# Mixing x on 64x64 quarters of TensorE, two blocks at a time, in a fused attention and FFN kernel on one Trainium2 core

## The reference, cut to what matters

```python
x = x + attention(mix(x, itok_B_0_15, L0_cond_weights))
x = x + ffn(quantized_linear(x, condB_codebook))

def mix(x, condition, weights):            # x: (64, 32, 512)
    W = weights[condition]                 # (64, 32, 32), one of 16 matrices for each batch entry
    return jnp.einsum('bct,bcd->bdt', x, W)
```

## Time and profile before

| | |
|---|---|
| median of 3 runs | 1451.32 us (1451.01 to 1451.55) |
| the profiled execution, its own time | 1450.27 us |
| span of that execution | 1448.4 us |
| PE busy | 1443.8 us, 100% of the span |
| PEld busy | 1200.6 us, 83% |
| DVE busy | 1079.1 us, 75% |
| ACT busy | 726.7 us, 50% |
| POOL busy | 746.3 us, 52% |

### The profile page before, as it was taken

How to read it: one execution, slowest core, us unless ns; L and a number is a source line. 1 busy time by engine, 2 the same in 40 slices (tenths; PEclk the granted TensorE clock), 3 DMA queues, 4 the chain that set the end, 5 groups by cost and what they waited for, 6 DMA issues and landing times.

```text
span 1448.4 us, 34721 instructions
## 1 busy us (share of the span) xinstructions
PE 1443.8 (100%) x14507; PEld 1200.6 (83%) x14507; DVE 1079.1 (75%) x1507; ACT 726.7 (50%) x1331; POOL 746.3 (52%) x530
## 2 busy tenths in 40 slices
PE   9999999999999999999999999999999999999999
PEld 8788888888888888888888888888888888888887
DVE  8788868687786777875478888867987667667663
ACT  7766676766766667676333333334432322222221
POOL 7668777777777877776345555514561111112100
PEclk9999999999999999999999999999999999999999
DMA  4211011110111011102443343447653334244230
GB/s 152 66 45 45 31 38 45 45 44 25 45 45 45 29 39 45 45 31 67 138 155 137 131 136 134 145 151 244 200 195 110 103 118 132 85 136 132 74 118 30
DMA packets 106989, 135.13 MB, mean 93 GB/s; under 512 B 6224, under 2 KB 89424, under 8 KB 106320
## 3 DMA queue, kind: packets, MB, share of 16 engines
q1 hardware_dynamic: 105968, 132.49, 27.7%
q10 hardware_dynamic: 864, 0.42, 0.1%
HBM read 86.75 MB, written 46.14 MB: 92 GB/s over the span
## 4 chain that ended last, share of the span: by engine, by line
PE 97%; DVE 1%; ACT 1%; DMA 0%; issue 0%; SPq 0%; DVEq 0%
PE bank L717 42%; PE bank L960 25%; PE bank L736 21%; PE bank L919 4%; PE bank L845 3%; PE bank L988 1%; PE bank L1006 1%; DMA qk<-in_x_nat 0%; PE bank L666 0%; DVE qreg L1708 0%; PE bank L1017 0%; PE bank L974 0%; ACT xs_hi L1160 0%; DVE wa L1624 0%; DVE sqst L1708 0%
## 5 line engine op out<-in xcount | busy, mean ns | idle before, releaser
L717 PE MATMUL bank<-xs_hi,wa 128*128 128x512 f32 x1792 | 563.3, 392 | 0.1
L1527 POOL TENSOR_TENSOR accr<-accr,sqst 128x512 f32<-128x512 f32 x248 | 353.2, 1435 | 147.7 <-ACT sqst L1197 107.5
L717 PEld LDWEIGHTS bank<-xs_hi,wa 128*128 128x128 f32 x1792 | 336.3, 188 | 74.1 <-DVE qk L1775 2.3
L717 PE MATMUL bank<-xs_lo,wa 128*128 128x512 f32 x896 | 348.7, 389 | 0.0
L960 PE MATMUL bank<-ot,wo_main 128*128 128x512 f32 x1344 | 316.4, 392 | 0.0
L960 PEld LDWEIGHTS bank<-ot,wo_main 128*128 128x128 f32 x1344 | 249.5, 188 | 52.6
L736 PE MATMUL bank<-wv,xs_hi 128*128 128x512 f32 (+1 forms) x1008 | 282.6, 366 | 0.1
L1624 DVE TENSOR_TENSOR wa<-wraw,wa 128x256 fp32r<-128x256 f32 (+1 forms) x160 | 157.0, 982 | 96.7 <-ACT wa L1106 95.0
L1322 ACT ACTIVATE ot<-bank,vec 128x256 fp32r<-128x256 f32 x256 | 100.3, 476 | 239.0 <-PE bank L960 146.6
L736 PEld LDWEIGHTS bank<-wv,xs_hi 128*128 128x128 f32 x1008 | 182.1, 189 | 32.9 <-issue 1.9
L717 PEld LDWEIGHTS bank<-xs_lo,wa 128*128 128x128 f32 x896 | 168.3, 188 | 33.2
(11 more groups left out here) (224 smaller groups left out, 1726.9 us busy)
## 6 DMA issues: line engine op xcount, KB each, us to landing
values_b<-v_spill SPq DMA_DIRECT2D x60, 512.0 KB, 4.9
wraw<-in_wqk SPq DMA_DIRECT2D x32, 512.0 KB, 3.5
v_spill<-qk SPq DMA_DIRECT2D x64, 256.0 KB, 2.3
v_spill<-sqst SPq DMA_DIRECT2D x64, 256.0 KB, 2.2
score_spill<-sqst SPq DMA_DIRECT2D x32, 256.0 KB, 2.0
wraw<-in_wv SPq DMA_DIRECT2D x16, 512.0 KB, 5.1
wraw<-score_spill SPq DMA_DIRECT2D x16, 512.0 KB, 4.0
spare<-in_wo SPq DMA_DIRECT2D x15, 512.0 KB, 4.8
```

What stands on the lines that cost most here:

```text
L717: ins = pe.matmul(dst[:, :], wa[:, col:col + P], xpart[:, j - 1, kt, n * CH:(n + 1) * CH], start=(first and k == 0), stop=(k == 5), skip_g ...
L1527: pool.tensor_tensor(a, a, sq_slot(count), ALU.add).then_inc(acc_done, 1)
```

## The change

The four 32x32 blocks of a tile's `mixw` lie inside its two diagonal 64x64 blocks. The change leaves out the two off-diagonal 64x64 parts, which are zero, and cuts each of the others once more by its features: `mix_tile(block, half, t)` does one half of a tile's tokens (64 rows of the array, 64 moving columns) as two matmuls of 64 stationary columns, for the lower and the upper 64 features. A matmul of before is four matmuls now, each on one 64x64 quarter of the array.

`mix_pair(one, other)` does two blocks at a time. For each of the four tiles it issues the upper rows of `one` (two quarters, one bank) and the lower rows of `other` (two quarters, another bank). Then PE waits on a semaphore of its own, `mix_crossed`, until all of that is done, and does the lower rows of `one` and the upper rows of `other`. Both blocks are reported to `mixed` at the end. `mix_group(3)` therefore waits for DVE's first difference before either of its first two blocks, and for t4 as well before either of its last two.

```diff
+            def mix_tile(block, half, t):
+
+                g, r, c, i = block
+                rows = slice(half * 64, (half + 1) * 64)
+                for d in range(2):
+                    ins = pe.matmul(mix_bank(g, r)[d * 64:(d + 1) * 64, t * P + half * 64:t * P + (half + 1) * 64],
+                                    x_in[c][rows, t, i * P + d * 64:i * P + (d + 1) * 64],
+                                    mixw[rows, c * TC + t, rows], start=True, stop=True)
+                return ins
+
+            def mix_pair(one, other):
+
                 for t in range(TC):
-                    ins = pe.matmul(mix_bank(g, r)[:, t * P:(t + 1) * P], x_in[c][:, t, i * P:(i + 1) * P],
-                                    mixw[:, c * TC + t, :], start=True, stop=True)
-                ins.then_inc(mixed, 1)
+                    mix_tile(one, 0, t)
+                    ins = mix_tile(other, 1, t)
+                ins.then_inc(mix_crossed, 1)
+                crossed[0] += 1
+                pe.wait_ge(mix_crossed, crossed[0])
+                for t in range(TC):
+                    first = mix_tile(one, 1, t)
+                    second = mix_tile(other, 0, t)
+                first.then_inc(mixed, 1)
+                second.then_inc(mixed, 1)
...
-                for i in range(KI):
-                    mix_block_of(i % 2, (0, 3)[i // 2] if c == 0 else (1, 2)[i // 2], c, i)
+                for i in (0, 2):
+                    r = (0, 3)[i // 2] if c == 0 else (1, 2)[i // 2]
+                    mix_pair((0, r, c, i), (1, r, c, i + 1))
...
                     pe.wait_ge(ld_x[1], 16)
-                    mix_block_of(g, 0, 1, kt)
-                    mix_block_of(g, 3, 1, kt + 2)
+                    mix_pair((g, 0, 1, kt), (g, 3, 1, kt + 2))
                     pe.wait_ge(ld_x[3], 16)
-                    mix_block_of(g, 1, 3, kt)
-                    mix_block_of(g, 2, 3, kt + 2)
+                    mix_pair((g, 1, 3, kt), (g, 2, 3, kt + 2))
                 else:
                     pe.wait_ge(x_act, x_act_at(2, 1))
-                    mix_block_of(g, 1, 3, kt)
                     pe.wait_ge(x_dve, x_dve_at(2, "t1"))
-                    mix_block_of(g, 0, 1, kt)
+                    mix_pair((g, 1, 3, kt), (g, 0, 1, kt))
                     pe.wait_ge(x_dve, x_dve_at(2, "l3"))
-                    mix_block_of(g, 2, 3, kt + 2)
                     pe.wait_ge(x_dve, x_dve_at(2, "t4"))
-                    mix_block_of(g, 3, 1, kt + 2)
+                    mix_pair((g, 2, 3, kt + 2), (g, 3, 1, kt + 2))
```

More of the change, by code:

```diff
@@ L336, in build @@
         mixed = sem("mixed")
+        mix_crossed = sem("mix_crossed")
         x_act = sem("x_act")
@@ L662, in _ @@
             warm_up(2)
-            def mix_block_of(g, r, c, i):
-                for t in range(TC):
-                    ins = pe.matmul(mix_bank(g, r)[:, t * P:(t + 1) * P], x_in[c][:, t, i * P:(i + 1) * P],
-                                    mixw[:, c * TC + t, :], start=True, stop=True)
-                ins.then_inc(mixed, 1)
+            crossed = [0]
+            def mix_tile(block, half, t):
[7 more added lines that the diff above has]
+            def mix_pair(one, other):
+                for t in range(TC):
+                    mix_tile(one, 0, t)
[8 more added lines that the diff above has]
+                second.then_inc(mixed, 1)
             def mix_chunk(c):
```

## The result

| | before | after |
|---|---|---|
| median | 1451.27 us (1450.19 to 1452.22, 15 runs) | 1454.28 us (1453.66 to 1454.98, 15 runs) |
| span of the profiled execution | 1448.4 us | 1453.2 us |
| PE busy | 1443.8 us | 1442.6 us |
| matmul records on PE | 14507 | 14891 |
| DVE, ACT busy | 1079.1, 726.7 us | 1081.4, 726.4 us |

The change is slower: +3.0 us, ratio 1.0021 with a 95% interval of 1.0013 to 1.0029. The forecast was 0.7 us faster.

A forecast was written before the change was run, and what follows sets the result against it. PE bounds the program (97% of the span), but ACT and DVE most of the mixing; so only 0.7 us of PE's 4.8 saved arrives. From the median of 1451.32 that gives 1450.6 us, range 1449.4 to 1452.8.

The forecast's parts named there:

- Four quarters at once: In PE's mixing, all four array quarters work together: a round 0.056 us, a pair of blocks 1.20 us instead of 1.80.
- The rival with two quarters at once: In the mixing only two quarters work together: a round 0.112, a pair 2.04 us, result 1453.5 us; chance 5%.
- The floor of 25 ns: PE starts at most one record per 25 ns: a round of the mixing 0.10 us, result 1452.8 us; chance 2%.
- How much of that arrives: Following the pairs, block (0, 1) starts on ACT 0.70 us earlier, and only that 0.70 reaches p1(2).
- the steps on pairs in groups 2 and 3: mix_group(2) takes 2.4 for 3.6 us, the surplus lost in waits; mix_group(3)'s second pair waits for t4, until 26.8.
- the cost of fetching the instructions: The change adds no transfer but that of instructions; the sum has no term for it.
- Instructions come too late: Three more instruction packets, about 1 us each; PE waits for one or two before pair 3: 1451.6 to 1452.6; chance 3%.
- The clock: Clock falls in PE's new pauses of 1.3 us; p1(0) and p2(0) take 2.75 us more: 1453.4; chance 2%.
- The sum: -0.7 us in 1450.27 us of the profiled execution, 1450.6 us against the median; nothing after the mixing is touched.
- The later steps of the forecast: p6(0) gains 1.4 us, p7(0)'s wait takes the surplus, group 3's waits leave the squares 0.7 us earlier.

The follow-up runs named there:

- chunk0_pairs: Kernel before with pairs on quarters for chunk 0 alone, eight warm-up matmuls left out, 23 tiny matmuls added in group 3; 1450.71 us beside 1451.35.
- the two variants: chunk0_pairs, and the same with the loads of chunks 1 and 3 issued only once the first pair is mixed; 1450.71 and 1450.51 us.
- pad16: Kernel before with 16 tiny matmuls (64 instructions) added after the gathering of the mixing matrices; 1466.31 us, +16.0.
- pause_cold: Kernel before with PE waiting for chunk 1 of x ahead of chunk 2's blocks, the array idle; 1455.27 us, +5.0.
- late_phased: late_pairs with 32 tiny matmuls (128 instructions) added in mix_group(3) where PE waits for DVE; 1451.34 us, +1.0 against the kernel before.
- late_pairs: Changed kernel with pairs for groups 2 and 3 only, chunks 0 and 2 on the full array as before; 1455.16 us beside 1451.55 for before.

## Why the prediction was wrong

**Right, by its own steps.** Four quarters at once: a pair was put at 1.20 us and takes 1.26, its first at 1.40 until ACT and is there 8.13 - 6.63 = 1.50 after it began. The rival with two quarters at once, and the rule of the Trainium skill behind it ("TensorE: Matmul & The Clock Gate", Part 3), would have made a pair 2.04. The floor of 25 ns on the same page would have made it some 1.85 (64 x 0.025 and the 0.25 of the rival); here 62 records start within 1.22 us, 20 ns apiece. That little of PE's time arrives is right too: where nothing stood in the way, in `chunk0_pairs`, p1(2) came 0.66 us earlier for the 0.70 that was said (the step "How much of that arrives"). The medians of the two variants moved by 0.6 and 0.8 us, with intervals that hold zero. Both have pairs in chunk 0 alone, so the steps on pairs in groups 2 and 3 were not tested by them; of those the changed kernel shows the gaps ahead of p6(0), 0.63 us at 24.49, and inside `mix_group(3)`, 0.25 at 30.67.

**The step that failed** is the cost of fetching the instructions. In the sum it stands at nothing: "It adds no work on another engine, and no transfer but that of instructions", and no term for that transfer follows. It was left to the rival "Instructions come too late (3%)", which had it wrong in its size, its chance and its evidence. The runs showed a stop of 4.08 us, and 2.15 to 4.70 in the variants that ran out at the start, in place of the 1 us for a packet.
- It priced a late packet at 1 us, the time that its bytes are under way. The time from asking to having is what counts, and that the rows of 0.3% of 16 engines don't tell. The trace of before had a better row, the small loads that were issued at about 2 us into the same full DMA engines (kernel before, DMA issues from 0 to 16 us; the last column is the median us to landing):

```profile
vec<-in_vecs ACTq DMA_DIRECT2D x1, 80.0 KB, 9.1
...
sl<-in_scale_log ACTq DMA_DIRECT2D x1, 8.0 KB, 8.0
```

  8 KB took 8.0 us. A fetch of 16 KB at 7 or 8 us had no reason to be quicker. The first packet of the kernel before itself moved only between 11.2 and 12.5 us (kernel before, DMA queues of that stretch, `q8 instruction: 1, 0.02, 5.3%`), and that of the changed kernel between 11.2 and 12.4. It was as late before, and nobody was waiting for it.
- It said that the scores ran through faster than this without a stop. They did because the boundaries of blocks fell well for them; `pad16` has the same scores with five stops. The absence of a stop in one trace was taken for spare capacity.
- It never counted. The changed kernel needs 132 + 512 records and loads by the end of chunk 2, where the kernel before has 445 of them up to 28.5 us, and one fetch in that time at its leisure. The Trainium skill has the missing figure ("Runtime: NRT & Kernel Launch", section "Instruction fetch mechanics"): instructions come in blocks of 256, 16 KiB each. The trace agrees, with 16.4 KB a packet and stops 256 k apart. The same section gives PE room for 2048 of them; by that figure there would have been no stop after 449, and here the measurement decides: stopping after 449 fits room for 512, two blocks, if some 60 instructions were issued before the first record (not shown). It also fits another sentence of that section, which has two lines of 16 KiB.

**The clock** was a rival of its own at 2%, for the pauses of 1.3 us that the forecast itself made. It fell in the stop instead, as a consequence of the other rival. The two are not alternatives to be weighed singly: a stop of some microseconds brings both bills. The price of 2.7 us was for the first two products at the low clock; what ran slow was the mixing. Where the clock fell, in the profiled `pause_cold`, it cost 2.6 at p1(2), so the price was about right and the chance was not.

**The sum**, put again with what was measured at the block that starts DVE's row of work: 11.60 before; pair 3 would have begun at 9.5, and did begin at 9.2, since chunk 2 landed sooner (7.4 us after its issue for 7.8); then 1.4 for the pair until ACT, the stop of 4.08, and about 0.8 for the low clock in what was left of the pair (36 records from 13.91 until ACT at 15.62, 1.7 us for some 0.9) make 15.5 from 9.2, and ACT began at 15.62. The later steps of the forecast (p6(0), p7(0), group 3 absorb and don't add) were on that chain in the same way: the delay of 4.0 at block (0, 1) is one of 3.8 at p1(2).

## What to carry to other kernels

Cutting a matmul into quarters multiplies its instructions by four. Count the instructions that an engine issues up to each place, in blocks as large as the packets of the instruction queue, and ask how long a small transfer takes at that moment, not how long its bytes do; in this start-up, which fills the DMA engines, it was 8.0 us for 8 KB. A change in the number of instructions also shifts every later block boundary, so that an edit at the start can cost 16 us in a dense stretch hundreds of microseconds later (`pad16`), or save 2.6 (`late_phased`, which only adds work to `late_pairs`, has +1.0 for +3.6): compare variants with equal counts modulo a block, and look for waits on "issue" in lines that were not changed.

## What was not expected of the hardware

- 16 tiny matmuls, 0.5 us of work, made the kernel 16.0 us slower (`pad16`, 1.0112, 1.0097 to 1.0127).
- After a stop of 4.08 us, and of 3.46 in `pause_cold`, PE ran at half clock for 5 to 6 us. Stops of about 2 us did this too, but not each of them: in `pad16` the clock fell with the stops of 2.01 and 2.02 us and stayed at 1.00 with those of 2.13, 2.32 and 2.37. In `late_phased` the granted clock fell with no idle stretch over 0.6 us, in a stretch of many small matmuls and short waits: PE was busy for 0.50 of 1.00 us from 27 to 28 us and for 0.49 from 29 to 30, and the clock was 0.50 from 30 to 33. Why it fell there stays open.
- Whether PE asks for a block exactly when it has finished one, and why it went on 1.6 us after the packet's bytes were through in the changed kernel, was not tested.
